# Attention values of two head groups in one TensorE run, feature gate and second keys in one run, and all five engine orders laid anew

## The chip, the cores and the metric

The kernel runs on one core of a Trainium2 chip. The metric is the device time of one execution in microseconds (us): the median of several executions, 1136.91 for the kernel before. It is written in Bass: each engine has its own instruction list, and every wait between engines is a semaphore written by hand.

## What is computed

`x` is (4, 1024, 256). Two residual layers follow each other:

```python
x = x + xattn(layernorm(x), ctx, itok, ...)   # 16 heads of 16; every token picks 64 of 154 keys by index
x = x + ffn(layernorm(x), ...)                # gated linear attention, 8 heads of 64
# xattn: softmax over the 64 picks. The kernel counts how often each of the 154 keys is picked and adds
#        ln(count) to the score, -1e30 where the count is 0.
# ffn:   q1, k1, v = x@Wq, x@Wk, x@Wv ; q2 = x@Wqa@Wqb ; k2 = softmax(x@Wka@Wkb)
#        gk1, gk2 = log_sigmoid(x@Wg?a@Wg?b)/16 ; one of 4 experts per token (top 1 of softmax(x@We))
#        o = chunk_gla(q1,k1,v,gk1) + sum_e chunk_gla(q2*fac_e, k2*fac_e, v, gk2*mask_e)
#        g = x@Wga@Wgb ; o = rmsnorm(o)*norm_w * (g*sigmoid(g)) ; return o @ Wo
```

The gates' logarithms are summed over the tokens; the kernel takes them from the middle of a tile of 128 tokens, 64 each way, and a state passes from tile to tile inside a batch row.

## The kernel before, in words

There are 32 tiles of 128 tokens. The program is a loop of 37 turns; turn i works on tile i in stage l (loads, first layer norm), i-1 in stage a (index counting, query), i-2 in stage b (attention), i-3 in stage c (second norm, hidden features, router, gates), i-4 in stage d (linear attention), and i-5 in stage e (output). Each engine has one function per kind of turn: `*_first_tiles` for turns 0 to 5, `*_tiles` for turns 6 to 32 (27 turns), `*_last_tiles` for the last four. In it the pieces of six tiles stand interleaved, in an order written out by hand, and an engine goes through its list strictly in that order.

TensorE (`pe_tiles`, L1045) has 372 instructions a turn or so; a float32 product is two of them. Its products differ in the part of the array that they use, and the trace prints it: 128\*128 for the full array (transposes, scores, projections), 64\*128 for two row halves side by side (`half_pairs` L793, `half_rows` L800, `inner` L806), 128\*64 for two column halves (`kv_products`, `inner_outputs`, `dense_kv_products`, `state_outputs` at L862), 64\*64 (L867), and 128\*32 for four column strips (`values`, L735, printed as L739 and L743). The steady order is: gate products (L821), XM transposes, exponent transposes (L732, L733), scores (L720), query product (L703), q2 (L797), hidden features (L755), K2 transposes, values 0, `inner` (L810), logit transpose, exponent transposes, KG1T transposes, scores, v product (L782), values 1, `inner`, KG2T transposes, exponent transposes, scores, feature gate (`half_pairs` with WG, L797), KV products (L837), z features (L774), values 2, inner outputs (L854), z product (L769), exponent transposes, state outputs (L862, L867), values 3, router rows (L786 to L788), scores of the next tile, OT transposes, mean square (L1116), dense KV (L846), ON transposes, second keys (`half_rows` with WKB, L803), attention output (L749), ffn output (L873), q1 (L407), XN transposes, k1 (L407).

`values(t, g, pt)` makes the weighted values of one group of four heads: eight products into `OUTS`, one strip of PSUM bank MA, which ScalarE then copies to OT (four copies a turn, L1882, L1901, L1921, L1934) before the strip can be written again.

```python
def values(t, g, pt):                     # L735
    o, v = OUTS, VNOW[t // TPB % 2]
    for hh in range(GH):
        pe.matmul(o[VW * hh:VW * hh + VW, :], v[:, c:c + VW], pt[:, cols(GH)], start=True, ...)
    for hh in range(GH):
        last = pe.matmul(o[VW * hh:VW * hh + VW, :], v[:, h * VW:(h + 1) * VW], pt[:, cols(hh)], ...)
```

VectorE (`dve_tiles`, L1418) holds among others the score maxima (L727), the one-hot comparison and its weighting (HOT, L1455 and L1472), its sums (L713), the attention-mask products (AT, L1464, L1474), Q1 (L1445), XM (L1447), XN (L1504), and the two prefix sums of the gates into GSUM (`tensor_tensor_scan`, L1522 backwards and L1529 forwards), which stand at the turn's end. The second norm goes X1 (L1431), statistics, ScalarE's Ln and Exp, XM. ScalarE (`act_tiles`, L1836) holds exponents and copies out of PSUM; GpSimd (`pool_tiles`, L2164) element-wise work in SBUF, among it SG<-SG,LS (L2203), state decays and the masked queries QM; SyncE (`sp_tiles`, L2309) issues all DMAs, the query slabs QS (`q_slabs`, L709) among them.

Of the kernel before, what the change touches and what calls it, by code (L numbers as in the profile page):

```python
# [7 lines left out]
P = 128  # L8
# [73 lines left out]
def program(nc, x, idx, ctxT, consts, w_q, w_down, w_up, w_out, wa, wq, wk, wv, wqk_b, wk_b, wg_b, wg, wo, norm_w, out):  # L82
# [4 lines left out]
    with ExitStack() as ctx:  # L87
# [194 lines left out]
        s_c_x1b = sem("c_x1b")  # L282
# [4 lines left out]
        s_c_hidden_ps = sem("c_hidden_ps")  # L287
        s_c_hidden = sem("c_hidden")
# [47 lines left out]
        s_d_qm0 = sem("d_qm0")  # L336
# [21 lines left out]
        s_d_stated = sem("d_stated")  # L358
# [16 lines left out]
        k2_heads = MIDS.rearrange("p a (h d) -> p a h d", d=DK)  # L375
# [359 lines left out]
        def values(t, g, pt):  # L735
            o, v = OUTS, VNOW[t // TPB % 2]
            for hh in range(GH):
                c = HA * VW + g * P + hh * VW
                pe.matmul(o[VW * hh:VW * hh + VW, :], v[:, c:c + VW], pt[:, cols(GH)],  # L739
                          start=True, stop=False, skip_group_check=True)  # L740
            for hh in range(GH):
                h = g * GH + hh
# [133 lines left out]
        def pe_first_tiles(l, a, b, c, d, e):  # L876
            if c == 0:
                pe_v_rest()
# [4 lines left out]
            if b == 0:  # L883
                pe_c_rest()
# [1566 lines left out]
```

## Time and profile before

| | |
|---|---|
| median of 3 executions | 1136.91 us (1136.44 to 1137.9) |
| profiled execution | 1137.37 us, span of its instructions 1135.8 us |
| busy in the span | TensorE 1077.7, VectorE 978.7, ScalarE 933.8, GpSimd 686.0 us |
| granted TensorE clock | 0.988 in the mean |

The span is what the trace covers; 1.57 us of the profiled execution lie around it. A turn is the time from one instruction of the loop to the same one a turn later. In an order of time the columns are the start, the duration, the engine, the line and the operation. A printed duration of a TensorE instruction reaches into the next one's, since products are pipelined; the distance from start to start says what it takes of the engine's time.

### The profile page before, as it was taken

The numbers are of one execution on the slowest core, as the hardware profiler recorded it, in microseconds if no ns is written. First come the engines' busy times: TensorE is split into PE (matmuls) and PEld (weight loads), VectorE is DVE, ScalarE is ACT, GpSimd is POOL, SyncE is SP. The second block draws the span as 40 slices with busy tenths as digits, with TensorE's granted clock in tenths as the row PEclk, the third lists the DMA queues.
The fourth block names the chain that finished last, engine by engine and source line by source line (L and its number), as shares of the span: only waits on it lengthen the run. The fifth ranks groups of instructions, "written<-read, shape, count | busy, mean of one in ns | idle before, by whom it ended". The sixth has DMA issues, their size and how long they took to land.

```text
span 1135.8 us, 30935 instructions
## 1 busy us (share of the span) xinstructions
PE 1077.7 (95%) x11840; PEld 872.7 (77%) x11840; DVE 978.7 (86%) x2793; ACT 933.8 (82%) x2322; POOL 686.0 (60%) x707
## 2 busy tenths in 40 slices
PE   2879999999999999999999999999999999999986
PEld 1557888887888788778888887888787788888764
DVE  5679999998899999999999998999899999998652
ACT  2578888888888888888888898888889888888761
POOL 4266555577655556766655677565557666555553
PEclk9889999999999999999999999999999999999998
DMA  5432222223222222223212222222222222121111
GB/s 155 141 124 58 72 52 57 54 70 76 67 68 52 50 57 73 62 70 86 67 43 50 57 67 71 73 71 48 63 57 61 63 68 68 44 52 48 31 32 24
DMA packets 86857, 73.83 MB, mean 65 GB/s; under 512 B 34553, under 2 KB 71743, under 8 KB 86710
## 3 DMA queue, kind: packets, MB, share of 16 engines
q1 hardware_dynamic: 86278, 70.98, 24.4%
q8 instruction: 93, 1.52, 0.6%
q10 hardware_dynamic: 432, 0.89, 0.2%
q14 instruction: 54, 0.44, 0.1%
HBM read 37.43 MB, written 13.94 MB: 45 GB/s over the span
## 4 chain that ended last, share of the span: by engine, by line
PE 79%; DVE 8%; DMA 3%; POOL 3%; ACT 3%; SPq 2%; issue 1%; DVEq 0%; ACTq 0%
PE F L407 8%; PE F L862 5%; PE F L810 5%; PE TM L732 5%; PE F L401 5%; PE F L873 4%; PE F L782 4%; PE F L837 4%; PE TM L739 3%; PE F L797 3%; PE F L867 3%; PE SA L720 3%; PE F L821 3%; PE TM L749 3%; PE F L755 2%; PE F L854 2%
## 5 line engine op out<-in xcount | busy, mean ns | idle before, releaser
L727 DVE CUSTOM_DVE_ANT_0 SA<-SA,LNC 128x154 f32<-128x154 f32 x512 | 146.5, 346 | 16.2 <-PE SA L720 13.0
L2176 POOL TENSOR_TENSOR QREST<-QT,QPARTS 128x256 f32<-128x256 f32 x27 | 18.1, 672 | 174.6 <-ACT QPARTS L1872 174.6
L713 DVE TENSOR_REDUCE PACKED<-HOT 128x19 int32<-128x1216 bf16 x64 | 92.4, 1443 | 0.2
L2194 POOL TENSOR_TENSOR QM<-QD,ISEXPT 128x1024 f32<-128x1024 f32 x27 | 81.9, 3032 | 11.5 <-DMA QD<-QG 11.1
L732 PE MATMUL TM<-CONST,EXPS 128*128 128x128 f32 x512 | 84.5, 288 | 0.4 <-ACT OT L1781 0.4
L732 PEld LDWEIGHTS TM<-CONST,EXPS 128*128 128x128 f32 x512 | 73.9, 207 | 2.0 <-ACT OT L1781 0.7
L2166 POOL TENSOR_TENSOR LS<-LS,ZABS 128x1024 f32<-128x1024 f32 x27 | 64.0, 2371 | 13.5 <-ACT ZABS L1932 13.0
L727 DVE DVE_READ_ACCUMULATOR2_ANT MAXS<- 128x1 f32 x512 | 70.6, 138 | 0.0
L2174 POOL TENSOR_TENSOR LS<-LS,ZABS 128x512 f32<-128x512 f32 x27 | 34.5, 1279 | 54.9 <-ACT ZABS L1840 54.9
L720 PE MATMUL SA<-KNOW,QS 128*128 128x154 bf16 x512 | 56.0, 232 | 10.9 <-DMA KNOW<-k_dram 9.2
L407 PEld LDWEIGHTS F<-XMT,WQ 128*128 128x128 f32 x512 | 63.4, 196 | 2.7 <-issue 1.3
L862 PE MATMUL F<-QM,STATE 128*64 128x128 f32 x1024 | 63.0, 276 | 2.3 <-POOL QM L2235 1.2
L873 PE MATMUL F<-WO,OG 128*128 128x256 f32 x256 | 62.4, 388 | 2.2 <-DVE OG L1638 2.2
L407 PE MATMUL F<-XMT,WQ 128*128 128x128 f32 x512 | 64.5, 280 | 0.0
L2196 POOL TENSOR_TENSOR AT<-AT 128x1024 f32<-128x1024 f32 x27 | 64.1, 2375 | 0.0
L2197 POOL TENSOR_TENSOR QM<-QD,ISEXPT 128x1024 f32<-128x1024 f32 x27 | 64.1, 2375 | 0.0
L407 PE MATMUL F<-XMT,WK 128*128 128x128 f32 x512 | 62.9, 276 | 1.2 <-DVE OUT L1547 1.2
L837 PE MATMUL F<-VM,KG 128*64 128x128 f32 x1024 | 63.0, 276 | 0.8 <-DVE AT L1596 0.8
L862 PEld LDWEIGHTS F<-QM,STATE 128*64 128x64 f32 x1024 | 55.2, 137 | 8.4 <-issue 4.0
L407 PEld LDWEIGHTS F<-XMT,WK 128*128 128x128 f32 x512 | 59.7, 192 | 2.4 <-DVE OUT L1547 2.0
L782 PE MATMUL F<-WV,XMT 128*128 128x512 f32 x128 | 61.3, 601 | 0.0
L837 PEld LDWEIGHTS F<-VM,KG 128*64 128x64 f32 x1024 | 55.3, 137 | 4.8 <-ACT KG L2036 1.0
(541 smaller groups left out, 3813.2 us busy)
## 6 DMA issues: line engine op xcount, KB each, us to landing
QD<-QG SPq DMA_DIRECT2D x128, 128.0 KB, 2.3
QS<-q_dram SPq DMA_DIRECT2D x64, 192.0 KB, 3.3
q_dram<-QPARTS SPq DMA_DIRECT2D x32, 192.0 KB, 2.4
XA<-x_dram SPq DMA_DIRECT2D x32, 128.0 KB, 2.1
QS<-q_dram SPq DMA_DIRECT2D x32, 128.0 KB, 3.3
XB<-x_dram SPq DMA_DIRECT2D x32, 128.0 KB, 3.2
out_dram<-OUT SPq DMA_DIRECT2D x32, 128.0 KB, 1.7
EG<-EGP SPq DMA_DIRECT2D x128, 4.0 KB, 1.8
```

The source lines that it names most:

```text
L407: last = pe.matmul(bank[:, cols(p)], lhs(k, p), rhs(k), start=k == 0, stop=k == contraction - 1)
L713: return dve.tensor_reduce(PACKED[:, r], HOT[:, r, :], AX.X, ALU.add)
L720: last = pe.matmul(SA[:, i, j * NKV:(j + 1) * NKV], QS[t % 2][:, slot, :], KNOW[t // TPB % 2][:, slot, :], start=True, stop=True, skip_gro ...
L727: last = dve.tensor_tensor_reduce(s, s, LNC[t % 2][:, :], -1.0, LARGE, ALU.add, ALU.min, out[:, h:h + 1])
L732: pe.transpose(TA[:, cols(hh)], exps[:, 0:P, hh], ident)
L782: last = pe.matmul(C0, xmt[:, k, :], WV[:, k, :], start=k == 0, stop=k == KD - 1)
L837: last = pe.matmul(o, KG2[:, h * DK:(h + 1) * DK], vm[:, h, ep, :, :].rearrange("p e d -> p (e d)"), start=True, stop=True)
L862: pe.matmul(D0[DK * par:DK * par + DK, cols(p)], STATE[:, par, p, e, :], QM[:, e, par, p, :], start=False, stop=False, skip_group_check=True)
L873: last = pe.matmul(out, og[:, p, :], WO[:, p, :], start=p == 0, stop=p == NP - 1)
L2194: pool.tensor_tensor(QM[:, 1, :, :, :].rearrange("p a b t -> p (a b) t"), QD[:, :, :, :].rearrange("p a b t -> p (a b) t"), ISEXPT[d % 2][ ...
L2196: pool.tensor_tensor(AT1[:, :, :, :], AT1[:, :, :, :], AT2[:, :, :, :], ALU.add).then_inc(s_d_at, 1)
L2197: pool.tensor_tensor(QM[:, 0, :, :, :].rearrange("p a b t -> p (a b) t"), QD[:, :, :, :].rearrange("p a b t -> p (a b) t"), ISEXPT[d % 2][ ...
```

## The change

It does four things, and the orders of all five engines are laid anew around them.

1. `values_pair` does two head groups one after the other, into two strips (`OUTS2`); four runs a turn become two, and ScalarE's four copies become two of twice the width. A group's maxima, exponents and transposes come earlier than its values, so both exponent buffers and both PT buffers are full before a run.
2. The feature gate (WG) and the second keys (WKB) stand behind each other in one run, late in the turn; the second keys go to another part of the same banks (`KIDS`). ScalarE's gate work (SG copy, Abs, Exp, Relu) moves to the turn's end with it.
3. The two scans, the key maximum and the product OG\*RMS move from the end of the turn to the start of the next, and the first three read stage d's buffers instead of c's.
4. GpSimd's SG product and the copy X1B move from the turn's end to right behind ScalarE's sigmoid exponent (`s_c_sigm`) in its first third; OFF moves to the turn's end, and one index step to the start of the next.

```diff
-        OUTS = MA[:, 3 * P:4 * P]
+        OUTS2 = MA[:, 2 * P:4 * P].rearrange("p (n t) -> p n t", t=P)
-        MID, MIDS, MIDD = D2[:, 0:D], F[:, 0:2, 0:D], F[:, 2:4, 0:D]
+        MID, MIDS, KIDS, MIDD = D2[:, 0:D], F[:, 0:2, 0:D], F[:, 0:2, D:2 * D], F[:, 2:4, 0:D]
-        def values(t, g, pt):
+        def values_pair(t, first):
+            v = VNOW[t // TPB % 2]
+            for n in range(2):
+                g, o, pt = first + n, OUTS2[:, n, :], PT[n]
+                for hh in range(GH):
+                    c = HA * VW + g * P + hh * VW
+                    pe.matmul(o[VW * hh:VW * hh + VW, :], v[:, c:c + VW], pt[:, cols(GH)],
+                              start=True, stop=False, skip_group_check=True)
+                for hh in range(GH):
+                    h = g * GH + hh
+                    last = pe.matmul(o[VW * hh:VW * hh + VW, :], v[:, h * VW:(h + 1) * VW], pt[:, cols(hh)],
+                                     start=False, stop=True, skip_group_check=True)
+        def half_pairs_rows(pairs_out, rows_out, w_pairs, x0, x1, w_rows, y1, y0):
+            half_pairs(pairs_out, w_pairs, x0, x1)
+            return half_rows(rows_out, y0, y1, w_rows)
```

The steady turn of TensorE afterwards, `pe_tiles`, its products in order and the waits that the prediction speaks of:

```diff
+            pe.wait_ge(s_c_xm, c + 1)
+            transposes(C0, XM[:, :], KD).then_inc(s_c_xmt_ps, 1)
+            pe.wait_ge(s_c_sigm, d + 1)
+            gate_products(LS3[d % 2], CUME[d % 2]).then_inc(s_d_g2_ps, 1)
+            pe.wait_ge(s_b_exps, 4 * b + 1)
+            scores(b, 1).then_inc(s_b_scores, 1)
...
+            q_product().then_inc(s_a_q_ps, 1)
...
+            pe.wait_ge(s_d_k1, d + 1)
+            pe.wait_ge(s_d_ep2, d + 1)
+            half_pairs(MIDD, WQKB, HQ[d % 2], HQ[d % 2]).then_inc(s_d_q2_ps, 1)
...
+            hidden(XMT[c % 2]).then_inc(s_c_hidden_ps, 1)
+            exp_transposes(EXPS[:, 0]).then_inc(s_b_exps_ps, 1)
+            pe.wait_ge(s_b_exps2_1, b + 1)
+            scores(b, 2).then_inc(s_b_scores, 1)
+            pe.wait_ge(s_d_q2, d + 1)
+            inner(KG1T, Q1).then_inc(s_d_a1_ps, 1)
...
+            transposes(D0, flat(K2[d % 2][:, :, :]), NP).then_inc(s_d_k2t_ps, 1)
...
+            pe.transpose(C0[:, 0:P], HID2[:, :], ident).then_inc(s_c_logit_ps, 1)
...
+            exp_transposes(EXPS[:, 1]).then_inc(s_b_exps_ps, 1)
...
+            v_product(XMT[c % 2]).then_inc(s_c_v_ps, 1)
...
+            transposes(D0, flat(KG1T[:, :, :]), NP).then_inc(s_d_k1t_ps, 1)
...
+            scores(b, 3).then_inc(s_b_scores, 1)
...
+            inner(KG2T, QG2).then_inc(s_d_a2_ps, 1)
...
+            transposes(D0, flat(KG2T[:, :, :]), NP).then_inc(s_d_k2gt_ps, 1)
+            values_pair(b, 0).then_inc(s_b_values, 1)
...
+            kv_products(VM[d % 2])
...
+            exp_transposes(EXPS[:, 0]).then_inc(s_b_exps_ps, 1)
...
+            z_features().then_inc(s_c_z0_ps, 1)
...
+            inner_outputs(V[d % 2]).then_inc(s_d_o_inner, 1)
...
+            exp_transposes(EXPS[:, 1]).then_inc(s_b_exps_ps, 1)
...
+            z_product(1).then_inc(s_c_z1_ps, 1)
...
+            state_outputs().then_inc(s_d_o_ps, 1)
...
+            scores(a, 0).then_inc(s_b_scores, 1)
...
+            router_rows().then_inc(s_c_rows_ps, 1)
+            values_pair(b, 2).then_inc(s_b_values, 1)
...
+            pe.matmul(D2, const("pairs"), RMS[:, :], start=True, stop=True).then_inc(s_d_ms_ps, 1)
...
+            transposes(TA, flat(OT[:, :, :]), GROUPS).then_inc(s_b_ot_ps, 1)
+            dense_kv_products(V[d % 2]).then_inc(s_d_kvd_ps, 1)
+            pe.wait_ge(s_c_hidg, 16 * c + 16)
+            pe.wait_ge(s_c_hidk, 16 * c + 16)
+            pe.wait_ge(s_c_cume, c + 1)
+            half_pairs_rows(MIDS, KIDS, WG, HID2, HIDG, WKB, HID1, HIDK).then_inc(s_c_k2_ps, 1)
...
+            transposes(TA, ON[:, :], KD).then_inc(s_b_ont_ps, 1)
...
+            ffn_out(MID, OG).then_inc(s_e_y_ps, 1)
...
+            attn_out().then_inc(s_b_y_ps, 1)
...
+                transposes(spare, XN[:, :], KD).then_inc(s_a_xt_ps, 1)
+            pairs(D1, lambda k, p: WQ[:, k, cols(p)], lambda k: XMT[c % 2][:, k, :], KD).then_inc(s_d_q1_ps, 1)
...
+            pairs(D2, lambda k, p: WK[:, k, cols(p)], lambda k: XMT[c % 2][:, k, :], KD).then_inc(s_d_k1_ps, 1)
```

VectorE's turn afterwards, in order: OG\*RMS, IW, scan backwards, IW, key maximum, scan forwards, K2 difference, OUT, X1, BASE, statistics, maxima 0, aggregate, key sum, Q1, XM, HOT comparison (L1455 before), KG1T, maxima 1, HOT weighting, reciprocal, QG2, K2 scaling, PT0, maxima 2, KG2T, AT1, statistics, maxima 3, AT2, half of the HOT sums, PT0, the other half, counts, XN, states, HQ, TRIE, OG\*SG, ISEXP, ISEXPT, CUME, RSUM, ON, STATED. ScalarE ends its turn with Ln and Exp of RMS, one VM copy, SG copy, Abs, ONT copy, Exp, Relu, and EP, and begins the next with EG, Ln of ZABS, Exp of K2, EN1, WEIGHT, XNT copy, the two small steps of RSTD2, the sigmoid exponent, and then four EXPS in a row. SyncE issues HIDK and HIDG between the second and the third query slab; both stood earlier.

```diff
 def pool_tiles
-            pool.tensor_tensor(SG[d % 2][:, :], SG[d % 2][:, :], LS3[d % 2][:, 2, :], ALU.mult).then_inc(s_c_sg, 1)
-            pool.tensor_copy(X1B[d % 2][:, :], X1[d % 2][:, :]).then_inc(s_c_x1b, 1)
+            pool.wait_ge(s_c_silu, 4 * d + 4)
+            pool.tensor_tensor(LS3[d % 2][:, 2, :], LS3[d % 2][:, 2, :], ZABS[:, 2, :], ALU.add).then_inc(s_c_ls2, 1)
+            pool.wait_ge(s_c_sigm, d + 1)
+            pool.tensor_tensor(SG[d % 2][:, :], SG[d % 2][:, :], LS3[d % 2][:, 2, :], ALU.mult).then_inc(s_c_sg, 1)
+            pool.tensor_copy(X1B[d % 2][:, :], X1[d % 2][:, :])
```

## Rows read from the trace of the kernel before

**Rows 1.** The page of the profile, parts 1 and 2: busy time, granted TensorE clock by slices.

```profile
PE 1077.7 (95%) x11840; PEld 872.7 (77%) x11840; DVE 978.7 (86%) x2793; ACT 933.8 (82%) x2322; POOL 686.0 (60%) x707
...
PEclk9889999999999999999999999999999999999998
```

**Rows 2.** Busy time in stretches: us, then busy us (instructions) of each engine, clock, DMA.

```profile
342.86:375.72 32.86, 32.67 (x370) 26.66 (x369) 30.25 (x87) 28.82 (x72) 19.86 (x22) 1.00 0.24 59
180.00:1048.00 868.00, 861.80 (x9687) 705.54 (x9687) 795.20 (x2292) 762.10 (x1900) 544.99 (x546) 1.00 0.25 62
```

**Rows 3.** The chain that ended last: start us, us, what; two turns apart.

```profile
339.20 1.90 PE F L862 x32
372.16 1.90 PE F L862 x32
```

**Rows 4.** TensorE's instructions in order of time, one middle turn: start us, us, what.

```profile
342.05 0.43 PE L739 MATMUL TM<-PT,VNOW 128*32 128x128 f32 x8
342.62 0.32 PE L786 MATMUL F<-CONST,RT 128*128 128x128 f32 x1
...
345.31 0.44 PE L401 MATMUL TM<-CONST,ON 128*128 128x128 f32 x2
345.81 0.45 PE L803 MATMUL F<-WKB,HIDK 64*128 64x256 f32 x1
...
346.48 1.13 PE L749 MATMUL TM<-WOUT,ONT 128*128 128x256 f32 x4
...
349.17 1.95 PE L407 MATMUL F<-XMT,WQ 128*128 128x128 f32 x16
350.96 0.38 PE L401 MATMUL F<-CONST,XN 128*128 128x128 f32 x2
351.18 1.95 PE L407 MATMUL F<-XMT,WK 128*128 128x128 f32 x16
353.21 1.17 PE L821 MATMUL F<-CUME,LS 128*128 128x136 f32 x8
...
357.95 0.60 PE L401 MATMUL F<-CONST,K 128*128 128x128 f32 x4
358.48 0.43 PE L739 MATMUL TM<-PT,VNOW 128*32 128x128 f32 x8
...
359.06 1.16 PE L810 MATMUL F<-Q,KG1T 64*128 64x128 f32 x16
360.15 0.33 PE L1068 MATMUL F<-CONST,HID 128*128 128x128 f32 x1
```

**Rows 5.** VectorE and GpSimd around the same turn, in order of time.

```profile
340.40 1.27 POOL L2203 TENSOR_TENSOR SG<-SG,LS 128x512 f32<-128x512 f32 x1
...
342.16 0.69 DVE L1506 TENSOR_TENSOR STATE<-STATE,F 128x512 f32<-128x512 f32 x1 [0.34 <-PE F L867]
...
346.50 0.68 DVE L1527 TENSOR_TENSOR OG<-OG,RMS 128x512 f32<-128x512 f32 x1
...
352.39 0.67 DVE L1445 SCALAR_TENSOR_TENSOR Q<-F,EP 128x512 f32<-128x512 f32 x1
...
352.99 0.39 DVE L1447 TENSOR_SCALAR XM<-X,MV,RSTD 128x256 f32<-128x256 f32 x1
```

**Rows 6.** VectorE's writers of GSUM and XN: duration ns min/median/max, first and last start.

```profile
L1522 DVE TENSOR_TENSOR_SCAN GSUM<-RESET,LS x27: 671/673/675, 180.9 to 1037.9; 128x256 f32<-128x256 f32 x27
L1529 DVE TENSOR_TENSOR_SCAN GSUM<-RESET,LS x27: 998/1001/1004, 182.4 to 1039.4; 128x256 f32<-128x256 f32 x27
...
L1643 DVE TENSOR_TENSOR_SCAN GSUM<-RESET,LS x2: 692/692/693, 1072.4 to 1101.6; 128x256 f32<-128x256 f32 x2
...
L1504 DVE TENSOR_SCALAR XN<-XA,MV,RSTD x26: 404/1350/1373, 175.8 to 999.9; 128x256 f32<-128x256 f32 x26
```

**Rows 7.** VectorE's groups by line, 190 to 1045 us: busy us, mean ns | idle before.

```profile
L1455 DVE TENSOR_TENSOR HOT<-BASE,BASETAB 128x2496 bf16<-128x2496 bf16 x26 | 37.5, 1442 | 0.0
```

**Rows 8.** SyncE's queue in the same turn: issue of the query slabs.

```profile
368.14 0.89 SPq L709 DMA_DIRECT2D QS<-q_dram  x2
```

More of the change, by code:

```diff
@@ L733, in exp_transposes @@
             return pe.transpose(MA[:, 0:P], exps[:, P:NPAD, :].rearrange("p j h -> p (j h)"), ident)
-        def values(t, g, pt):
[L736 to L742, printed above, removed]
-                last = pe.matmul(o[VW * hh:VW * hh + VW, :], v[:, h * VW:(h + 1) * VW], pt[:, cols(hh)],
-                                 start=False, stop=True, skip_group_check=True)
+        def values_pair(t, first):
[10 more added lines that the diff above has]
+                                     start=False, stop=True, skip_group_check=True)
             return last
@@ L1175, in pe_last_tiles @@
             if b < TILES:
-                pe.wait_ge(s_b_probs_act, 2 * b + 1)
-                values(b, 1, PT[1]).then_inc(s_b_values, 1)
+                pe.wait_ge(s_b_probs, 2 * b + 1)
+                exp_transposes(EXPS[:, 1]).then_inc(s_b_exps_ps, 1)
+            if c < TILES:
+                pe.wait_ge(s_c_hidden, 2 * c + 2)
+                v_product(XMT[c % 2]).then_inc(s_c_v_ps, 1)
             if d < TILES:
@@ L1447, in dve_tiles @@
             dve.tensor_scalar(XM[:, :], X1[c % 2][:, :], MV2[:, 0:1], RSTD2[:, 1:2], ALU.subtract, ALU.mult).then_inc(s_c_xm, 1)
+            dve.tensor_tensor(HOT[:, :, :], BASE[:, :].unsqueeze(1).to_broadcast([P, BASES, PICKS]), BASETAB[:, :, :], ALU.is_equal).then_inc(s_a_hot, 1)
+            dve.wait_ge(s_d_k1_ps, d + 1)
+            dve.tensor_tensor(flat(KG1T[:, :, :]), D2, EN1[:, :], ALU.mult).then_inc(s_d_k1, 1)
+            dve.wait_ge(s_b_scores, 4 * b + 2)
+            maxima(b, MAXS[:, 1, :]).then_inc(s_b_max, 1)
@@ L1453, in dve_tiles @@
-            dve.tensor_tensor(flat(KG1T[:, :, :]), D2, EN1[:, :], ALU.mult).then_inc(s_d_k1, 1)
-            dve.wait_ge(s_a_weights, 2 * a + 2)
-            dve.tensor_tensor(HOT[:, :, :], BASE[:, :].unsqueeze(1).to_broadcast([P, BASES, PICKS]), BASETAB[:, :, :], ALU.is_equal).then_inc(s_a_hot, 1)
-            dve.wait_ge(s_b_scores, 4 * b + 2)
-            maxima(b, MAXS[:, 1, :]).then_inc(s_b_max, 1)
+            dve.wait_ge(s_b_exps_ps, 4 * b + 1)
             dve.tensor_copy(PT[0][:, :], ROWS).then_inc(s_b_probs, 1)
-            dve.wait_ge(s_d_q2_ps, d + 1)
@@ L1534, in dve_last_tiles @@
+            if b < TILES:
+                dve.wait_ge(s_a_counts_pool, b + 1)
+                maxima(b, MAXS[:, 0, :]).then_inc(s_b_max, 1)
+            dve.wait_ge(s_e_y_ps, e + 1)
+            dve.wait_ge(s_e_store, 16 * e)
+            dve.tensor_tensor(OUT[:, :], MID, X1B[e % 2][:, :], ALU.add).then_inc(s_e_out, 1)
             if c < TILES:
@@ new lines, in act_tiles @@
+            act.activation(WEIGHT[:, 0:PICKS - 1], IW[5][:, 0:PICKS - 1], ACT.Exp, scale=float(DIGIT * np.log(2.0))).then_inc(s_a_weights_act, 1)
+            act.wait_ge(s_a_xt_ps, a + 1)
+            act.activation(XNT[:, :, :], spares, ACT.Copy).then_inc(s_a_xt, 1)
+            act.wait_ge(s_d_exp1, 3 * d + 1)
+            act.activation(middle(EP), const("ident")[:, 0:NP], ACT.Exp, scale=0.0).then_inc(s_d_ep1m, 1)
+            act.wait_ge(s_c_ln, 2 * c + 2)
+            act.activation(RSTD2[:, 0:1], MV2[:, 1:2], ACT.Ln, bias=eps).then_inc(s_c_rstd, 1)
```

1433 lines of the change are left out of this document (669 added, 764 removed).

## The prediction, made before the change was run

> **What bounds the kernel now.** I began with the page: TensorE is busy 95% of the span at a granted clock of 9 or 10 tenths in every slice, its upper level of 2.4 GHz, and VectorE 86% [rows 1]. Both are near full, so the question is which one sets a turn. The table of stretches answers for the middle: in a turn of 32.86 us TensorE is busy 32.67, VectorE 30.25, ScalarE 28.82, GpSimd 19.86, and over the 868 us from 180 on TensorE is 99% busy [rows 2]. The chain that ended last shows the same state product 32.96 us apart in neighbouring turns, and nothing but TensorE between most of them [rows 3]. So a turn lasts what TensorE's list takes. But "busy" hides two things, which only the starts in the order of time show [rows 4]. Sixteen full-array instructions of 128 columns take 1.79 us (349.17 to 350.96), 0.112 each. The second such sixteen take 2.03 (351.18 to 353.21): 0.24 is a wait for Q1, which VectorE ends at 353.06 [rows 5]. The two ON transposes take 0.50 where XN's two take 0.22, which is another wait. Second, where the used part of the array changes, some time goes: four transposes before the values take 0.53 instead of 0.45; the values, sixteen instructions in four strips and so four deep, 0.58 instead of 0.45; `inner`, sixteen in pairs, 1.09 instead of 0.90 [rows 4].
>
> **The change, part by part.** *Changes of the array's part.* I count them in the printed lists. Before: q2 2, values with `inner` 3 and 3, feature gate with KV 3, values with inner outputs 3, state outputs (two parts) with values 4, dense KV 2, second keys 2: 22. After: q2 2, `inner` 2 and 2, values pair with KV 3, inner outputs 2, state outputs 3, values pair 2, dense KV with gate and keys 3: 19. So six merged or separated runs give only three fewer, because the old values mostly stood beside a run that needed a change anyway. Price of one: 0.08, 0.13 and 0.19 by the three excesses above, mean 0.13; the second keys' 0.67 against 0.45 gives an upper end of 0.22. Three are 0.40 us a turn (0.24 to 0.66). The products stay the same in number and columns.
>
> *The old waits.* 0.24 before the gate products, and 0.28 less one change (0.13) before the second keys: 0.39 a turn. The first goes, since XM comes after Q1 on VectorE and now the XM transposes go first; the second, since the keys wait for CUME and stand 0.9 us later. What is late next, I count from the end of the state outputs, S (342.05). Before, the gate products begin at S+11.16 and XM ends at S+11.33 (352.99 and 0.39 [rows 5]). After, TensorE has in that stretch one more values group and the feature gate (0.45 each), one change less (0.13) and no old waits (0.39): it stands at XM's transposes at S+11.54. VectorE has the same work there (two small steps of K2 leave it, BASE comes in, about 0.2 either way), still begins 0.11 after S, but RSUM and STATED come up against the later OT transposes and dense KV, about 0.15 each; that puts XM at S+11.6, or at S+11.3 if the forward scan is quicker (below). ScalarE's small steps for the norm are due at S+11.1 behind the gate work (five instructions of 512 columns) that moved to this stretch, which I lay with some doubt. So the two arrive together; I take 0.1 of waiting, ends 0 and 0.4.
>
> *Later in the turn.* q2 waits for the last of two exponents out of the gate products, which stand behind four EXPS in a row: 0.1. The third scores wait for four EXPS that follow the second maxima: 0.1. The values pair has both PT buffers early; KV products wait for AT2, whose cover is the pair itself (1.0 us); if it went, AT2 would be up to 0.4 late. The second PT0 copy now waits about 1 us for the transposes, an idle that VectorE can afford: 30.25 of 32.4 us, less 0.9 if XN runs free. New waits together 0.3, ends 0 and 0.9.
>
> *The scans and XN.* The forward scan takes 1.001 us in each of 27 turns and 0.692 in the two last, the backward one 0.673 always; XN takes 404 ns at best and 1350 in the median, while GpSimd's SG product of 1.27 us runs beside it [rows 5, 6]. Moving SG and the scans can give VectorE back 0.31 + 0.95. It is not the bound, so I count only what it does for XM above. The Trainium skill (SBUF — State Buffer, section "SBUF: two separate sides") would have either scan, with two SBUF inputs, block against a GpSimd instruction that reads SBUF; the trace agrees for the forward scan and shows no such case for the backward one, and by the rule the sum would be the same.
>
> *ScalarE and SyncE.* Two wide OT copies for four small ones save ScalarE some 0.3 us beside other work: nothing. SyncE puts two HID copies ahead of the last query slab; two issues of 0.45 (0.89 for two [rows 8]) against a last issue at 369.0 and scores that need it at 375.8: 6.8 us of cover, so nothing. Without the cover it would be 0.9 a turn.
>
> *Sum.* 0.40 + 0.39 - 0.30 = 0.49 us a turn, 32.37 instead of 32.86. 27 turns are of the steady kind, and two of the fill run as full; 29 x 0.49 = 14.2 us. Fill and drain have the same work in a new order: 0, ends -4 and +4. The span goes from 1135.8 to 1121.6, the profiled execution (1.57 around it) from 1137.4 to 1123.2; the median of the runs shown lies 0.46 lower, so **1123 us**. The forecast's own bounds: at worst 0.24 + 0.39 - 0.60 a turn, which is about 1136; at best 0.66 + 0.39 - 0.1, about 1109.
>
> **The rivals.** *A, slower: the HOT comparison loses the port.* After XM VectorE starts the HOT comparison (1.44 us [rows 7]); at nearly that moment, right behind the sigmoid exponent, GpSimd starts the SG product that it used to do late. XN shows what happens to a VectorE instruction that comes second: up to 0.95 us more [rows 6]. By my laying HOT starts at S+11.6 and SG at S+11.7, too near to call. If SG is first, HOT, KG1T and the second maxima come up to 1.27 later; q2 waits for KG1T, which was to end at S+13.8 against q2's start at S+14.5, so 0.6 of the wait shows, and the third scores, with no such slack, show up to 1.2. I take 0.9 more per turn: 32.37 + 0.9 = 33.27, 0.41 over the old turn, x 29 = 12: 1149 us. It decides from the point where SG precedes HOT in every turn. For it: XN's median; against: sigmoid stands behind RSTD2's last step, so XM and HOT may have gone first. The skill's section named above calls it an exclusive lock in which the loser fully blocks, and the trace agrees with XN's numbers. *B, same:* the saved changes turn into waiting of the same size, since VectorE's chain from S to XM was as long as TensorE's: 0.79 of new waits, 1137 us. For it: 353.38 against 353.21 above. *C, more:* VectorE gains 0.31 in the scan and arrives early, no new waits, and a change costs more than 0.13 (0.17): 0.51 + 0.39 = 0.90 a turn, 1111 us. That the change does not do what it says has no room: the merged runs are in the list.
>
> **How the numbers follow.** Forecast 0.52, A 0.22, B 0.13, C 0.13. A measurement of this kernel tells about 0.2% (2.3 us) from no change. Faster by more takes forecast, C and 0.04 of B: 0.69. Within it: 0.08. Slower: A and 0.01 of B, 0.23. The range takes the forecast, B, most of C and the lower third of A: 1108 to 1143.
>
> **What would show it.** Right: turns of 32.2 to 32.5 us between equal state products; values runs of about 1.0 us for 32 instructions twice a turn; 2.03 gone from the k1 products; XN near 0.4 and the forward scan near 0.69. Wrong: XM's transposes starting more than 0.4 after k1's sixteen should be over; a HOT comparison of over 2 us or starting with GpSimd's end (A); turns of 32.8 (B).

## The result, and the profile after the change

| | before | after |
|---|---|---|
| median of 4 executions, us | 1136.82 | 1152.84 (1150.46 to 1154.34) |
| profiled execution / its span, us | 1137.37 / 1135.8 | 1152.80 / 1151.5 |
| busy TensorE / VectorE / ScalarE / GpSimd, us | 1077.7 / 978.7 / 933.8 / 686.0 | 1055.7 / 968.8 / 896.6 / 701.9 |

The ratio is 1.0137, with a 95% interval of 1.0119 to 1.0156: the changed kernel is 1.4% slower. The forecast was 1123 with a range to 1143 and 0.23 on slower. It was wrong in sign and outside its range.

The page after, parts 1 and 2 (before: [rows 1]):

```profile
PE 1055.7 (92%) x11840; PEld 872.4 (76%) x11840; DVE 968.8 (84%) x2793; ACT 896.6 (78%) x2258; POOL 701.9 (61%) x707
...
PE   2558999999999999999999999999999999999985
...
PEclk8869999999999999999999999999999999999999
```

One steady turn of the changed kernel, busy time as in [rows 2]:

```profile
353.05:386.23 33.18, 32.16 (x372) 26.80 (x370) 29.87 (x87) 27.57 (x71) 21.51 (x22) 1.00 0.23 58
```

TensorE, busy 32.67 of 32.86 us before, is now busy 32.16 of 33.18: its own work got shorter and a microsecond of idleness came in. Where it waits, by the view of waits (TensorE, 190 to 1060 us):

```profile
PE F L797 <- DVE KG1T L1437: 13.8, 26, 0.5
PE SA L718 <- ACT EXPS L1844: 12.7, 26, 0.5
```

TensorE has two waits in each of 26 turns, before q2 and before the third scores. Measured from start to start they are 0.60 and 0.66 us, since a product's printed duration reaches into the wait. Both hang on VectorE, as the chain that ended last shows (before, TensorE alone stood in most of it [rows 3]):

```profile
331.29 2.45 DVE HOT L1435
333.74 0.60 DVE KG1T L1437
...
364.46 2.45 DVE HOT L1435
366.91 0.60 DVE KG1T L1437
```

The same turn in order of time, all engines (start, duration, what):

```profile
363.44 0.19 ACT L1823 ACTIVATE RSTD<-RSTD 128x1 f32<-128x1 f32 x1
363.46 0.68 DVE L1432 SCALAR_TENSOR_TENSOR Q<-F,EP 128x512 f32<-128x512 f32 x1
363.53 0.62 ACT L1825 ACTIVATE LS<-LS 128x512 f32<-128x512 f32 x1
364.05 0.41 DVE L1434 TENSOR_SCALAR XM<-X,MV,RSTD 128x256 f32<-128x256 f32 x1
364.23 1.37 POOL L2140 TENSOR_TENSOR SG<-SG,LS 128x512 f32<-128x512 f32 x1 [1.26 <-ACT LS L1825]
364.37 2.54 DVE L1435 TENSOR_TENSOR HOT<-BASE,BASETAB 128x2496 bf16<-128x2496 bf16 x1
365.54 1.63 POOL L2141 COPY X1B<-X 128x256 f32<-128x256 f32 x1
...
366.83 0.68 DVE L1437 TENSOR_TENSOR KG1T<-F,EN 128x512 f32<-128x512 f32 x1
...
367.62 0.71 PE L797 MATMUL F<-HQ,WQKB 64*128 64x128 f32 x8 [0.53 <-DVE KG1T L1437]
```

HOT starts 0.14 us behind the SG product and lasts 2.54 us instead of 1.44 [rows 7]: SG ends at 365.60, and from there to HOT's end at 366.91 are 1.31. GpSimd's next instruction, the X1B copy, meets HOT on its side and takes 1.63 instead of 0.46 (0.40 in e1, with nothing beside it). This is in every steady turn but the first one, and there HOT started 0.02 us ahead of SG, kept its 1.45, and it was SG that took 2.56 instead of 1.27:

```profile
166.36 1.45 DVE L1435 TENSOR_TENSOR HOT<-BASE,BASETAB 128x2496 bf16<-128x2496 bf16 x1
166.38 2.56 POOL L2140 TENSOR_TENSOR SG<-SG,LS 128x512 f32<-128x512 f32 x1 [1.59 <-ACT LS L1825]
```

The scans came out as hoped, and XN nearly so (before: [rows 6]). VectorE's writers of HOT, XN and GSUM, min/median/max in ns:

```profile
L1435 DVE TENSOR_TENSOR HOT<-BASE,BASETAB x27: 1453/2539/2545, 166.4 to 1028.4; 128x2496 bf16<-128x2496 bf16 x27
...
L1491 DVE TENSOR_SCALAR XN<-XA,MV,RSTD x26: 498/502/506, 185.8 to 1015.7; 128x256 f32<-128x256 f32 x26
...
L1412 DVE TENSOR_TENSOR_SCAN GSUM<-RESET,LS x27: 676/682/684, 161.3 to 1023.3; 128x256 f32<-128x256 f32 x27
```

**Where the 15.7 us of the span are.** I put the same product, the state outputs, of turn 5 and of turn 32 beside each other, 27 turns apart. Before:

```profile
141.02 1.97 PE L862 MATMUL F<-QM,STATE 128*64 128x128 f32 x32 [0.38 <-POOL QM L2146]
...
1031.43 1.97 PE L862 MATMUL F<-QM,STATE 128*64 128x128 f32 x32
```

After:

```profile
152.05 1.97 PE L866 MATMUL F<-QM,STATE 128*64 128x128 f32 x32
...
1047.33 1.97 PE L866 MATMUL F<-QM,STATE 128*64 128x128 f32 x32
```

Up to turn 5 the changed kernel loses 11.0 us, in the 27 turns 4.9 (33.16 against 32.98 each in the mean; the median turn goes from 32.86 to 33.17, and the mean differs less because the kernel before has a few longer turns, the longest of 34.46). Behind them it gains 0.2. The larger part is in the fill, the turns before the steady ones, which the forecast had put at 0 with ends of 4. Each of these figures comes from one profile, and e2 shows below how far a fill varies. TensorE's waits up to 130 us, after (the longest, 10.3 for XN, was 10.0 before and is left out):

```profile
...
PE TM L536 <- POOL CREST L525: 8.2, 1, 8.2
PE F L399 <- DVE XM L1286: 6.5, 1, 6.5
PE F L774 <- DMA ZW<-w_dram: 6.2, 1, 6.2
...
PE SA L718 <- DMA KNOW<-k_dram: 2.7, 1, 2.7
```

The wait for CREST was 1.1 us before the change, those for XM and ZW were not among the waits, and the one for KNOW was 9.2. SyncE's queue shows what feeds them, after:

```profile
19.76 0.42 SPq L2254 DMA_DIRECT2D IDX<-idx_dram  x1
...
44.48 1.05 SPq L2254 DMA_DIRECT2D IDX<-idx_dram  x1
...
75.73 1.90 SPq L682 DMA_DIRECT2D ZW<-w_dram  x3
```

and before:

```profile
10.21 0.43 SPq L2245 DMA_DIRECT2D IDX<-idx_dram  x1
...
25.65 0.43 SPq L2245 DMA_DIRECT2D IDX<-idx_dram  x1
...
51.14 0.91 SPq L684 DMA_DIRECT2D ZW<-w_dram  x3
```

In `sp_first_tiles` the new order has the index load near the turn's end instead of second, and the gate weight slabs right behind it, in turn 3 as before but so much later. GpSimd casts IDX in its own order, with CREST behind the cast; XM stands behind index steps on VectorE. Whether these chains cost the time is what e2, e6 and e7 ask.

### The profile page after: what moved, and what is told of

It reads as the page before. It is cut to its first block, busy times and chain, and to the rows that moved or that the text cites. A ratio compares the mean times of both kernels' runs of the same rounds, so it can differ in the third digit from the quotient of the medians.

```text
span 1151.5 us, 30649 instructions
## 1 busy us (share of the span) xinstructions
PE 1055.7 (92%) x11840; PEld 872.4 (76%) x11840; DVE 968.8 (84%) x2793; ACT 896.6 (78%) x2258; POOL 701.9 (61%) x707
## 4 chain that ended last, share of the span: by engine, by line
PE 65%; DVE 19%; ACT 7%; DMA 3%; POOL 3%; issue 2%; SPq 1%; DVEq 0%; POOLq 0%
DVE HOT L1435 6%; PE F L866 5%; PE F L814 5%; PE F L841 5%; PE F L877 5%; PE TM L730 5%; DVE SA L725 4%; PE F L782 4%; PE F L399 4%; PE TM L739 3%; PE F L871 3%; PE SA L718 3%; PE F L858 3%; PE F L1104 2%; PE TM L749 2%; PE TM L743 2%
## 5 line engine op out<-in xcount | busy, mean ns | idle before, releaser
L730 PE MATMUL TM<-CONST,EXPS 128*128 128x128 f32 x512 | 90.2, 299 | 4.3 <-ACT EXPS L1743 4.2
L1435 DVE TENSOR_TENSOR HOT<-BASE,BASETAB 128x2496 bf16<-128x2496 bf16 x27 | 67.5, 2499 | 0.0
L2159 POOL TENSOR_TENSOR QM<-QD,ISEXPT 128x1024 f32<-128x1024 f32 x27 | 64.1, 2373 | 0.7 <-DMA QD<-QG 0.7
L2143 POOL TENSOR_TENSOR QREST<-QT,QPARTS 128x256 f32<-128x256 f32 x27 | 26.1, 967 | 61.9 <-ACT QPARTS L1841 61.9
L2162 POOL TENSOR_TENSOR QM<-QD,ISEXPT 128x1024 f32<-128x1024 f32 x27 | 63.9, 2365 | 0.0
L718 PEld LDWEIGHTS SA<-KNOW,QS 128*128 128x128 bf16 x512 | 37.7, 99 | 33.4 <-ACT EXPS L1844 18.8
```

The source lines that it names most:

```text
L718: last = pe.matmul(SA[:, i, j * NKV:(j + 1) * NKV], QS[t % 2][:, slot, :], KNOW[t // TPB % 2][:, slot, :], start=True, stop=True, skip_gro ...
L730: pe.transpose(TA[:, cols(hh)], exps[:, 0:P, hh], ident)
L1435: dve.tensor_tensor(HOT[:, :, :], BASE[:, :].unsqueeze(1).to_broadcast([P, BASES, PICKS]), BASETAB[:, :, :], ALU.is_equal).then_inc(s_a_ho ...
```

## The experiments

Each ran beside the kernel before on the same chip, and the ratio is to that (medians of the kernel before 1136.3 to 1137.1). "Turn" is the time between the state outputs of turns 5 and 32, mean of 27 and median, and "fill" the start of those of turn 5; both come from the one profile of each run.

| | median us | ratio (95%) | turn, mean | turn, median | fill |
|---|---|---|---|---|---|
| before | 1136.82 | | 32.98 | 32.86 | 141.0 |
| after | 1152.84 | 1.0137 (1.0119 to 1.0156) | 33.16 | 33.17 | 152.1 |
| e1 SG behind HOT | 1131.4 | 0.995 (0.9933 to 0.9967) | 32.23 | 32.14 | 156.0 |
| e2 loads early | 1145.79 | 1.0077 (1.0053 to 1.0100) | 33.14 | 33.17 | 143.5 |
| e3 both | 1121.75 | 0.9869 (0.9842 to 0.9896) | 32.25 | 32.14 | 143.4 |
| e4 both, values split | 1130.27 | 0.994 (0.9918 to 0.9962) | 32.63 | 32.48 | 143.0 |
| e5 before, SG beside HOT | 1147.61 | 1.0100 (1.0079 to 1.0122) | 33.44 | 33.09 | 140.2 |
| e6 e1 and IDX early | 1123.52 | 0.9887 (0.9861 to 0.9913) | 32.27 | 32.14 | 148.7 |
| e7 e1 and ZW early | 1124.2 | 0.9898 (0.9874 to 0.9922) | 32.31 | 32.14 | 147.3 |
| e8 e3, SG late | 1120.87 | 0.9867 (0.9842 to 0.9893) | 32.31 | 32.17 | 142.9 |
| e9 e3, exponent transposes first | 1120.62 | 0.9853 (0.9832 to 0.9874) | 32.26 | 32.09 | 145.0 |
| e10 e2, KG1T before HOT | 1132.46 | 0.9949 (0.9932 to 0.9966) | 32.60 | 32.58 | 146.7 |
| e11 e3, copy beside HOT | 1122.5 | 0.9873 (0.9849 to 0.9897) | 32.37 | 32.31 | 141.8 |

**e1: take the SG product off HOT.**

```diff
 def pool_tiles
             pool.wait_ge(s_c_sigm, d + 1)
+            pool.wait_ge(s_a_hot, 2 * a + 1)
             pool.tensor_tensor(SG[d % 2][:, :], SG[d % 2][:, :], LS3[d % 2][:, 2, :], ALU.mult).then_inc(s_c_sg, 1)
```

> The kernel after the change, with one wait added in the steady turn: GpSimd starts the SG product (and the X1B copy behind it) only when VectorE's HOT comparison is over. Theory (the HOT comparison is held up by the SG product): HOT, 2.54 us in the median of the changed kernel, takes about 1.45 in all 27 turns; KG1T and the second maxima come 1.1 us earlier; of TensorE's two stalls of 0.60 (q2) and 0.66 (third scores) a turn about 0.16 is left; turn 33.17 - 1.1 = 32.07; 27 x 1.1 = 30 us, so about 1123 us. Rival 1 (the SG product then runs into the HOT weighting or QREST instead, and VectorE loses the same time there): HOT weighting 2.5, third scores still 0.6 late, turn 32.5 to 33.0, 1135 to 1148. Rival 2 (TensorE's stalls come from ScalarE's EXPS order and not from HOT): turn within 0.1 of 33.17, 1150 to 1153.

One wait added, and 21 us gone. VectorE's HOT in e1:

```profile
L1435 DVE TENSOR_TENSOR HOT<-BASE,BASETAB x27: 1447/1453/1455, 170.2 to 1008.2; 128x2496 bf16<-128x2496 bf16 x27
```

Neither the wait for KG1T nor the one for the third scores' EXPS is left among TensorE's waits of e1 between 190 and 1030 us; what is left before q2 is 0.15 us a turn for ScalarE's EP (4.0 us in 26 turns), as expected. The mean turn is 32.23, 0.93 less, and the median turn 32.14, 1.04 less, near the 1.1 expected. Rival 1 is out: the HOT weighting takes 1.50 us, where it took 1.45 in the changed kernel. Rival 2 is out by the turn.

The time came out at 1131, not at the 1123 expected. In the profile it fell by less than 27 x 0.93 = 25 because the fill was 3.9 longer (156.0 against 152.1) with the same instructions; TensorE's granted clock stands at 0.83 from 90 to 120 us there, where it was 1.00 in the changed kernel.

**e2: the two loads back.**

```diff
 def sp_first_tiles
             sp.dma_start(XA[:, :], x[rows(l), :]).then_inc(s_l_load_xa, 16)
+            if l >= 1:
+                sp.wait_ge(s_a_index, 5 * l - 4)
+            sp.dma_start(IDX[:, :], idx[rows(l), :]).then_inc(s_l_load_idx, 16)
+            if l == 0:
+                sp_first()
+            if c == 0:
+                sp_w_slabs()
...
-            sp.dma_start(IDX[:, :], idx[rows(l), :]).then_inc(s_l_load_idx, 16)
-            if l == 0:
-                sp_first()
-            if c == 0:
-                sp_w_slabs()
```

> The kernel after the change, with two issues of SyncE put back where they stood before the change, in the turns of the fill alone: the index load IDX second in its turn instead of near the end, and the gate weight slabs ZW right behind it. Theory (the fill's loss is these late loads): the waits of 8.2 us (CREST), 6.5 (XM) and 6.2 (ZW) on TensorE in the first 130 us go down to about 1 us in all; the state products of the second full turn, at 141.0 before the change and 152.1 after it, come back to about 141 to 144; 8 to 11 us less, 1142 to 1145 us. Rival (the new order of the compute engines in the fill costs it, and the loads only show as the last of several): less than 4 us back, 1149 or more. The steady turn stays at 33.17 by either.

TensorE's waits up to 130 us in e2, the first of them:

```profile
PE SA L718 <- DMA KNOW<-k_dram: 9.7, 1, 9.7
...
PE F L769 <- ACT LS L1759: 3.5, 1, 3.5
PE F L399 <- DVE XM L1286: 2.1, 1, 2.1
```

The waits for CREST and ZW are gone, XM's is 2.1, and the one for KNOW, which the late loads had covered, is back at 9.7 as before the change. The fill ends at 143.5, 8.6 us sooner in the profiles, and the median of the runs is 7.1 lower (1145.79, just above the range expected); the turn stays at 33.14.

How much of the 8.6 is the loads' is less sure than it looks, because the fill varies with TensorE's granted clock, which changes between its upper level (1.00, 2.4 GHz) and its lower one (0.50, 1.2 GHz) in the first 100 us. Seven runs have the same instructions there, new order and both loads early; in order of their mean granted clock from 82 to 90 us:

| | e11 | e8 | e4 | e3 | e2 | e9 | e10 |
|---|---|---|---|---|---|---|---|
| clock, 82 to 90 us | 1.00 | 0.92 | 0.91 | 0.88 | 0.88 | 0.59 | 0.50 |
| fill, us | 141.8 | 142.9 | 143.0 | 143.4 | 143.5 | 145.0 | 146.7 |

The lower the clock in this stretch, the longer the fill, by 4.9 us from one end to the other. The kernel before had 1.00 there and a fill of 141.0, 0.8 less than e11's at the same clock; the changed kernel had 0.51 and 152.1. So the changed kernel's fill in its one profile mixes late loads and a clock that rose late (after 89 us), and whether the late loads are themselves a reason for the late clock no run shows. The firm figure for the loads is that of the medians, about 7 us.

**e3: both.**

> Both edits at once: GpSimd's SG product behind the HOT comparison, and the loads IDX and ZW early in the fill. If both theories hold, the gains add, since one is in the fill and the other in the steady turns: 1152.8 - 30 - 10 = 1113 us, 2% under the kernel before. If only the first holds 1123, if only the second 1143.

The gains add: 21.4 from e1 and 7.1 from e2 would make 1124.3, the run gives 1121.75, 1.3% under the kernel before. The 1113 expected was too low: I had taken 1.1 for the turn where 0.91 came in the mean (5 us), and 10 for the loads where e2 gave 7 (3 us).

**e6 and e7: which load.** Each moves one of e2's two pieces, on top of e1.

> The changed kernel with the SG product behind HOT, and in the fill only the index load IDX put back early (gate weight slabs ZW stay late). With both loads early the gain was 9.7 us (1131.4 to 1121.75). Theory: IDX starts the chain that ends in CREST's and XM's waits (8.2 and 6.5 us), and the wait for ZW (6.2) stands behind it, so IDX alone gives 5 to 7 us: 1124 to 1127. Rival (ZW is what ends the fill, and IDX is hidden behind it): under 3 us, 1129 or more.

> The other half: only the gate weight slabs ZW early, IDX late. Theory: ZW's wait of 6.2 us goes but for the z slabs behind it: 3 to 5 us, 1126 to 1128. Rival: all 9 to 10 of it, 1122.

Against e1's median IDX alone gives 7.9 us, ZW alone 7.2, both together (e3) 9.7. In e6 the wait for ZW is still 6.3 us, in e7 those for CREST and XM are 7.7 and 6.8, so each load ends its own waits and no others. For e6 the median lies just under the range, for e7 it lies under it. Each alone brings most of what both bring, but the intervals of e6 and e7 overlap that of e3, so the rival of e7 (all of it) is not excluded, that of e6 (under 3 us) is. How the two gains add up stays open: counted in fills from e1's 156.0 they are 7.3, 8.7 and 12.6, from the changed kernel's 152.1, with the same late loads, 3.4, 4.8 and 8.7, which is nearly a plain sum.

**e5: the one move, in the kernel before.**

```diff
 def pool_tiles
             pool.tensor_tensor(LS3[d % 2][:, 2, :], LS3[d % 2][:, 2, :], ZABS[:, 2, :], ALU.add).then_inc(s_c_ls2, 1)
+            pool.wait_ge(s_c_sigm, d + 1)
+            pool.wait_ge(s_a_weights, 2 * a + 2)
+            pool.tensor_tensor(SG[d % 2][:, :], SG[d % 2][:, :], LS3[d % 2][:, 2, :], ALU.mult).then_inc(s_c_sg, 1)
...
-            pool.tensor_tensor(SG[d % 2][:, :], SG[d % 2][:, :], LS3[d % 2][:, 2, :], ALU.mult).then_inc(s_c_sg, 1)
```

> The kernel before the change, and of the change only this: in the steady turn GpSimd's SG product leaves the turn's end and stands behind its LS product, started by the sigmoid exponent and BASE, about 0.5 us before VectorE's HOT comparison. Theory (the product that comes first holds up the other): HOT 1.44 goes to about 2.2, XN from 1.35 to 0.40; the later VectorE work comes 0.75 later, and since TensorE is the bound of that turn and waits for QG2, KG2T and AT soon behind it, 0.3 to 0.75 a turn shows: 27 x 0.5 = 14, 1145 to 1157 us. Rival 1 (VectorE had slack there in the kernel before, its SA maxima and PT0 were early): HOT longer, time within 3 us of 1137. Rival 2 (no hold-up between these two as such; what the changed kernel showed came from ScalarE or the write port of HOT alone): HOT stays at 1.44.

HOT's row in e5, and the meeting in one turn:

```profile
L1455 DVE TENSOR_TENSOR HOT<-BASE,BASETAB x27: 2206/2214/2219, 156.3 to 1025.5; 128x2496 bf16<-128x2496 bf16 x27
```

```profile
355.49 0.68 DVE L1453 TENSOR_TENSOR KG1T<-F,EN 128x512 f32<-128x512 f32 x1
355.71 1.28 POOL L2177 TENSOR_TENSOR SG<-SG,LS 128x512 f32<-128x512 f32 x1 [3.38 <-DVE BASE L1450]
...
356.09 2.21 DVE L1455 TENSOR_TENSOR HOT<-BASE,BASETAB 128x2496 bf16<-128x2496 bf16 x1
```

The same product beside the same comparison costs the old kernel 0.46 us a turn in the mean (0.23 in the median turn; the rest is in ten turns that are 0.3 to 2.7 longer) and 11.3 us in all, although XN ran free (0.45 us in the median). KG1T, which reads PSUM and ran through the start of SG, kept its 0.68. SG ends at 356.99 and HOT at 358.30, again 1.31 later. So the hold-up needs nothing of the new order; the order only brought the two together.

**e10: leave GpSimd, put KG1T ahead of HOT.**

```diff
 def dve_tiles
-            dve.tensor_tensor(HOT[:, :, :], BASE[:, :].unsqueeze(1)..., BASETAB[:, :, :], ALU.is_equal).then_inc(s_a_hot, 1)
             dve.wait_ge(s_d_k1_ps, d + 1)
             dve.tensor_tensor(flat(KG1T[:, :, :]), D2, EN1[:, :], ALU.mult).then_inc(s_d_k1, 1)
+            dve.tensor_tensor(HOT[:, :, :], BASE[:, :].unsqueeze(1)..., BASETAB[:, :, :], ALU.is_equal).then_inc(s_a_hot, 1)
```

> The changed kernel with the early loads, GpSimd untouched (SG product still behind the sigmoid exponent, beside HOT), and on VectorE only KG1T put ahead of the HOT comparison. Theory (the hold-up costs only what stands behind it and is waited for): HOT still starts after SG and is still held, now for 0.5 us instead of 1.1 (about 1.9 us instead of 2.54); KG1T is on time, q2's wait is 0.15; the second maxima come 0.55 earlier than in the changed kernel but 0.5 later than with SG behind HOT, so the third scores still wait 0.3 to 0.4; turn 32.5 to 32.6 against 33.14, 14 to 17 us less than the 1145.8 of the same kernel without it: 1129 to 1132. Rival (all the loss is KG1T's place, or the maxima's): 1122, or 1140 and more.

HOT, and TensorE's waits from 190 to 1000 us, in e10:

```profile
L1437 DVE TENSOR_TENSOR HOT<-BASE,BASETAB x27: 1651/1655/1740, 161.8 to 1009.4; 128x2496 bf16<-128x2496 bf16 x27
```

```profile
PE SA L718 <- ACT EXPS L1844: 7.0, 25, 0.3
PE F L797 <- ACT EP L1835: 3.8, 25, 0.2
```

13.3 us of the 24 that e3 gives come without touching GpSimd. The median turn is 32.58, 0.59 less than e2's, where e3's is 1.04 less; of the 0.45 between them the third scores' wait shows 0.28 (7.0 us in 25 turns). HOT is held for only 0.2, since KG1T itself waited 0.19 for k1's products and HOT came later than I had laid it, about 1.0 us behind SG's start.

**e8: the SG product back at the turn's end.** It stands behind the index steps of GpSimd and ahead of OFF, with a wait for it ahead of VectorE's OG\*SG.

> The kernel of both edits (SG behind HOT, loads early; 1121.75 us, turn 32.20), and the SG product put back at the turn's end, beside VectorE's counts and XN, where it was before the change; the X1B copy stays behind HOT. Theory (moving SG off XN gave VectorE time, but TensorE is the bound): XN goes from 0.50 to about 1.3 us, VectorE's idle of 0.95 before STATE takes it up, the turn stays at 32.2, within 2 us of 1121.75. Rival (LABB behind XN is then late for the router rows): XN's 0.8 shows in part, 0.2 to 0.5 a turn, 5 to 14 us more.

VectorE's groups in e8, 190 to 1000 us (busy, mean ns | idle before):

```profile
L1479 DVE TENSOR_SCALAR COUNTI<-PACKED 128x39 int32<-128x39 int32 x25 | 20.0, 799 | 0.9
...
L1495 DVE TENSOR_TENSOR STATE<-STATE,F 128x512 f32<-128x512 f32 x25 | 17.0, 680 | 2.4 <-PE F L871 2.4
```

The expectation named the wrong victim: XN kept its 0.50, and a count of 39 columns was hit, 1.20 us instead of 0.19 in 16 of 27 turns. It ends 0.04 us behind SG (175.47 to 176.67 in the first of them, with SG from 175.35 to 176.63), so what is lost is the rest of GpSimd's instruction, however small VectorE's is. VectorE's idle before STATE went from 25.6 us in e3 to 2.4 and took up nearly all of it. The time is the same as e3's within the spread. So moving the product off XN, one aim of part 4 of the change, is worth nothing here; VectorE had the room at the turn's end and none behind XM.

**e11: only the copy beside HOT.** The X1B copy stands ahead of the wait for HOT, the SG product behind it.

> The kernel of both edits, and GpSimd's X1B copy (one input, 0.40 us) put right behind the sigmoid exponent, so that it starts about 0.1 us before the HOT comparison; the SG product still waits for HOT. Theory 1 (any GpSimd work in SBUF holds HOT up): HOT 1.6 to 1.8 instead of 1.45. Theory 2 (only the product with two inputs does, the copy gives way): HOT 1.45 and the copy stretched, as the copy behind SG was in the changed kernel (1.63 instead of 0.40). Time within 4 us of 1121.75 by either, since q2 and the third scores have almost no slack for 0.3: 0 to 0.15 a turn.

HOT and the copy in e11:

```profile
L1435 DVE TENSOR_TENSOR HOT<-BASE,BASETAB x27: 1452/1654/1656, 156.0 to 997.7; 128x2496 bf16<-128x2496 bf16 x27
```

```profile
L2140 POOL COPY X1B<-X x27: 498/503/1692, 156.0 to 997.6; 128x256 f32<-128x256 f32 x27
```

Theory 1: a copy with one input holds HOT as well, for 0.2; the median turn grows by 0.17, the time by less than its spread. The extremes of the two rows, 1.69 for a copy and 1.45 for a HOT, are one turn, in which HOT started at 156.00 and the copy at 156.02: who starts first is served. And in all four kernels in which HOT came second (the changed one, e5, e10, e11) it ends 1.31 to 1.32 us behind GpSimd's instruction in every such turn, however much of that was left when HOT started.

**e4: the price of a change of the array's part.**

```diff
 def pe_tiles
+            pe.wait_ge(s_c_zmin, 2 * c + 2)
+            values_pair(b, 2, (0,))
             pe.wait_ge(s_c_router, 5 * c + 4)
-            pe.wait_ge(s_c_zmin, 2 * c + 2)
             router_rows().then_inc(s_c_rows_ps, 1)
-            values_pair(b, 2).then_inc(s_b_values, 1)
+            values_pair(b, 2, (1,)).then_inc(s_b_values, 1)
```

> The kernel of both edits, and in its steady turn the second values pair split again: the first group's eight products and eight more, then the router rows (full array), then the second group. Nothing else is moved; two changes of the array's used part are added in a turn. Prediction's price, 0.13 us a change: start to start from the scores of the next tile to the mean-square product 0.26 us more a turn, 27 x 0.26 = 7 us more than the kernel of both edits. Rival 1 (a change costs 0.08 or less, the excess seen in rows is the four-deep strips themselves): under 4 us more. Rival 2 (a change costs 0.2): 11 us more. If waiting elsewhere takes it up (TensorE not the bound of the turn), the distance grows but the time does not.

TensorE in e3 and then in e4, from the scores to the mean square:

```profile
339.82 0.44 PE L718 MATMUL SA<-KNOW,QS 128*128 128x154 bf16 x4
...
341.37 1.13 PE L1104 MATMUL F<-RMS,CONST 128*128 128x512 f32 x2
```

```profile
341.67 0.44 PE L718 MATMUL SA<-KNOW,QS 128*128 128x154 bf16 x4
...
342.62 0.32 PE L786 MATMUL F<-CONST,RT 128*128 128x128 f32 x1
...
343.51 1.13 PE L1105 MATMUL F<-RMS,CONST 128*128 128x512 f32 x2
```

1.84 against 1.55 us (1.836 and 1.554 in the median of 25 turns): 0.28 for two changes, 0.14 each, where the forecast had 0.13. This is the price of going to the four column strips and back; changes between other parts were not measured by themselves. The mean turn grew by 0.38 and the time by 8.5 us; the 0.1 beyond the two changes I have not traced (the router rows come later for VectorE, and GpSimd's QM is waited for in some turns).

**e9: fill TensorE's last wait.** The exponent transposes move from behind the hidden features to ahead of q2.

> The kernel of both edits (1121.75 us, turn 32.20), and TensorE's first exponent transposes moved ahead of q2, so that they fill its last wait (0.15 us a turn for ScalarE's EP). Theory: that wait goes, the third scores then come 0.05 to 0.1 too early for their EXPS; 0.05 to 0.15 a turn less, 1.5 to 4 us, 1118 to 1120 us. Rival: the third scores' wait takes all of it, time unchanged within 1 us.

The wait before q2 (4.0 us in 26 turns of e3) is gone from the waits, but the third scores take it up: from the hidden features' start to theirs are 1.16 us (421.09 to 422.25), where e3 has 0.99 up to the next products (354.65 to 355.64). The median turn is 0.04 shorter, the mean 32.26 against 32.25, and the time 1.1 us lower, which is within the spread of the runs; so the rival is about right. e3, e8 and e9 cannot be told apart; each beats both kernels.

## Why the prediction was wrong, point by point

**Rival A came true, and its price was right; its chance was wrong.** It said 0.9 us a turn through HOT, KG1T and the second maxima, with 0.6 before q2 and up to 1.2 before the third scores. The traces have 0.60 and 0.66, and taking it away gives 0.93 a turn in the mean and 1.04 in the median (e1); HOT lasted 1.10 longer, where A had up to 1.27. The step that failed is the laying of the two starts: "HOT starts at S+11.6 and SG at S+11.7". They came at S+11.32 and S+11.18 (S, the end of the state outputs, is 353.05 here). Both engines were earlier than laid, ScalarE by more: the norm's last step, "due at S+11.1", ended at 363.63, S+10.58, and the sigmoid exponent and SG follow from it alone. VectorE could have been first only if XM had started right at that step's end: XM's 0.32 from start to start would have put HOT at 363.95, ahead of SG's 364.23. But XM stands behind Q1, and Q1 (363.46, 0.68 us) kept VectorE until XM's start at 364.05. The forecast had VectorE arrive just with TensorE, so without such a lead; on its own laying the 0.1 between two starts carried a sign that an error of 0.5 in ScalarE's place turns. With so small a distance the chance of A had to be near a half, not 0.22, and its 0.9 us a turn more than took the forecast's gain.

What the Trainium skill states in SBUF — State Buffer, section "SBUF: two separate sides", is an exclusive lock for the whole instruction, with the loser fully blocked. The trace agrees in both directions (HOT behind SG 2.54 us, SG behind HOT 2.56 in the one turn where HOT was first), and e8 shows it with a victim of 0.19 us. One meeting does not fit it, the backward scan's beside OFF (below); there the measurement decides. The prediction cited the Trainium skill for the scans, where it changed nothing, and in rival A; it did not use it to go through every meeting that the change creates and to order their starts.

**The fill: "0, ends -4 and +4" failed, by 11 us.** The forecast said that fill and drain "have the same work in a new order", costed SyncE's moves for the steady turn alone (the two HID copies, which indeed cost nothing), and never laid `sp_first_tiles`. There a load went from second place to nearly last, so that it was issued 9.6 and 18.8 us later in turns 1 and 2. Two issues put back bring 8.6 of the 11.0 in the profiles, and 7.1 us in the medians (e2). The other 2.4 are within what the same instructions vary by from profile to profile (4.9 us, in the order of the granted clock): e11, with e2's fill and the clock at 1.00 from 82 us on as in the kernel before, ends it at 141.8, 0.8 behind that kernel.

**The steady sum without A had the right terms and was low.** With A and the late loads taken out (e3), the median turn is 32.14 against 32.86 before: 0.72 saved (0.73 in the mean), where the forecast had 0.49 and a turn of 32.37. Its terms: the three changes 0.42 by e4's price, if the others cost the same (0.40 forecast); the old waits, 0.39, all but gone (k1's sixteen take 1.85 us up to the next products instead of 2.03, the ON transposes 0.27 instead of 0.50); new waits 0.15 before q2 and none before the third scores, where 0.3 had been taken. That is 0.66; the last 0.06 I can't place. The term that was mis-sized is thus the new waits. The values pair is 1.01 us for 32 instructions, as said, and the XM transposes began at S+11.47 against S+11.54. That e3's 1121.75 lies so near the 1123 forecast is partly luck: its steady saving is half as large again, and its fill is 2.4 us longer where the forecast had 0. The forecast's bounds did not follow its terms either: its new waits had the ends 0 and 0.9, and the bounds were worked out with 0.1 and 0.6.

**Rivals B and C.** B (waits that eat the saving) had no place of its own: the waits that came are A's. C (0.17 a change, no new waits, 1111 us) had the price too high (0.14) and missed the q2 wait, but its turn of 31.96 is nearer to e3's 32.14 than the forecast's 32.37: VectorE did arrive early.

**Scans and XN.** The forward scan went from 1.001 to 0.682, as forecast to be free, and XN from 1.350 to 0.502 us, where near 0.4 was forecast; that they are worth nothing, since VectorE is not the bound, holds too; e8 shows it for the place of the SG product, while the scans were not moved back by themselves. The time that VectorE got back there (0.32 and 0.85) is about the time it lost behind XM (1.10), and only the second had someone waiting. The prediction expected the lock to meet either scan and saw no such case for the backward one. The trace before has the two side by side and no hold-up: the backward scan ran from 180.91 to 181.59 beside GpSimd's OFF, which ran from 180.65 to 181.41, and kept 0.68, while the forward one took 1.00 beside LNC (182.14 to 182.88).

## What to carry to other kernels

Before an element-wise instruction moves to GpSimd's next free place, write down what VectorE runs in that stretch and who waits behind it; the instruction that comes second loses the rest of the first one's duration (about 0.1 less than that in these traces), so the stretch to choose is one where VectorE is about to be idle. Where two starts hang on one event, add up what each engine still has between it and the start, from the rows, before calling it even.

A new order has to be costed in the fill function by function, loads first: a load that moves behind waits in SyncE's list delays every engine that takes its first use in order, and 7 us lost there are as much as 0.26 us in each of 27 turns. Before a fill of two profiles is compared, their granted clocks have to be put beside each other.

## What was not expected of the hardware

A VectorE instruction of 39 columns (0.19 us) took 1.20 us beside GpSimd's product of 1.28. GpSimd's plain copy of one tensor holds VectorE's comparison too (0.2 us in e11), and is itself held by it (1.63 instead of 0.40). The one that comes first is not quite untouched: SG took 1.37 instead of 1.27 in the changed kernel and the copy 0.50 instead of 0.40 in e11, yet SG kept 1.28 in e5; why is open. KG1T, with one operand in PSUM, was not held in e5 (0.68 us; 0.67 in the kernel before). XN took 0.50 us beside GpSimd's OFF, which started 0.04 us behind it, in the changed kernel and 0.404 at best before; what makes these 0.1 is open. VectorE's backward scan was not held beside OFF, and the forward one was beside LNC; which GpSimd instructions hold VectorE was not tested further.
